# A selective-scan loop: rates spread from bf16 parts, both drives and both sums ahead of the rates in each step, and half of a convolution moved to VectorE

## What is computed

```python
xm, z = split(rmsnorm(x) @ W_in.T)
u     = silu(causal_depthwise_conv(xm, conv_w) + conv_b)      # 4 taps along the tokens
dt, Bm, Cm = split(u @ W_x.T)
delta = softplus(dt @ W_dt.T + b_dt)
A     = -exp(A_log)                                           # (512, 64)
for t in range(32):                                           # per sequence
    h = exp(delta[t][:, None] * A) * h + (delta[t] * u[t])[:, None] * Bm[t][None]
    y[t] = h @ Cm[t]
out = (y + u * Dp) * silu(z) @ W_out.T + x
```

## Time and profile before

| | us |
|---|---|
| median of 3 runs | 1955.35 (1955.21 to 1955.81) |
| the profiled execution | 1953.92 |
| its span, first to last instruction | 1952.1 |

### The profile page before, as it was taken

How to read it: one execution, slowest core, us unless ns; L and a number is a source line. 1 busy time by engine, 2 the same in 40 slices (tenths; PEclk the granted TensorE clock), 3 DMA queues, 4 the chain that set the end, 5 groups by cost and what they waited for, 6 DMA issues and landing times.

```text
span 1952.1 us, 24426 instructions
## 1 busy us (share of the span) xinstructions
PE 1711.4 (88%) x9096; PEld 821.3 (42%) x9096; DVE 1011.8 (52%) x1520; ACT 761.7 (39%) x1201; POOL 703.1 (36%) x430
## 2 busy tenths in 40 slices
PE   7888886898999999999997759999812979899998
PEld 4666663542322332332333525444401557644443
DVE  2444444255888888888884333222359464522121
ACT  1333332196676666666661222111413240112121
POOL 0433330215998998998995010000000014000000
PEclk8999997798999999999999768999865879789999
DMA  2111101002000100100100600111062100101110
GB/s 68 32 32 32 32 27 52 0 8 96 12 12 7 29 12 7 29 12 7 29 6 17 223 1 0 33 48 32 5 143 70 33 0 1 44 1 43 44 43 21
DMA packets 36491, 65.63 MB, mean 34 GB/s; under 512 B 13509, under 2 KB 22617, under 8 KB 34981
## 3 DMA queue, kind: packets, MB, share of 16 engines
q1 hardware_dynamic: 33204, 63.42, 11.0%
q10 hardware_dynamic: 3200, 1.07, 0.2%
HBM read 55.80 MB, written 8.67 MB: 33 GB/s over the span
## 4 chain that ended last, share of the span: by engine, by line
PE 80%; DVE 12%; ACT 2%; DMA 2%; issue 2%; POOL 1%; SPq 1%; DVEq 0%; ACTq 0%; POOLq 0%
PE ps L845 17%; PE ps L888 7%; PE ps L1376 6%; PE ps L2123 6%; PE ps L2112 6%; PE ps L860 5%; PE ps L201 4%; PE ps L1389 3%; PE ps L342 3%; PE ps L347 3%; PE ps L224 3%; PE ps L360 2%; DVE arena L477 2%; PE ps L1887 2%; PE ps L1903 2%
## 5 line engine op out<-in xcount | busy, mean ns | idle before, releaser
L1156 POOL TENSOR_TENSOR arena<-arena 128x768 f32<-128x768 f32 x248 | 521.5, 2122 | 75.2 <-DVE arena L1106 45.0
L845 PE MATMUL ps<-arena 32*128 32x512 f32 x2016 | 368.7, 647 | 2.9 <-DMA arena<-m_bd 2.9
L1106 DVE TENSOR_TENSOR arena<-arena,ps 128x1024 f32<-128x1024 f32 x248 | 302.0, 1218 | 11.7 <-POOL arena L1156 5.5
L845 PEld LDWEIGHTS ps<-arena 32*128 32x128 f32 x2016 | 130.0, 184 | 194.2 <-issue 165.2
L1086 DVE TENSOR_TENSOR arena<-arena,ps 128x1024 f32<-128x1024 f32 x124 | 151.4, 1221 | 87.5 <-PE ps L845 87.5
L1012 ACT ACTIVATE arena<-arena 128x1024 f32<-128x1024 f32 x124 | 131.0, 1057 | 166.1 <-DVE arena L1086 166.1
L2069 POOL TENSOR_TENSOR arena<-arena 128x1024 f32<-128x1024 f32 x16 | 29.9, 1896 | 435.0 <-DVE arena L2002 421.7
L888 PE MATMUL ps<-arena 128*32 128x512 f32 (+15 forms) x1024 | 136.2, 604 | 9.4 <-DVE arena L1106 8.9
L1019 ACT ACTIVATE arena<-ps 128x1024 f32<-128x1024 f32 x124 | 127.0, 1024 | 19.7 <-PE ps L845 3.4
L1021 ACT ACTIVATE arena<-arena 128x1024 f32<-128x1024 f32 x124 | 131.1, 1057 | 3.9
L1376 PE MATMUL ps<-arena 128*128 128x512 f32 x288 | 131.8, 602 | 0.6 <-ACT arena L1441 0.6
(11 more groups left out here) (291 smaller groups left out, 2345.3 us busy)
## 6 DMA issues: line engine op xcount, KB each, us to landing
arena<-ctxT SPq DMA_DIRECT2D x32, 257.0 KB, 3.0
arena<-ctxT SPq DMA_DIRECT2D x8, 1028.0 KB, 15.2
arena<-L_ffn_w SPq DMA_DIRECT2D x16, 512.0 KB, 4.3
arena<-ctx_rows SPq DMA_DIRECT2D x8, 960.0 KB
m_rows<-arena SPq DMA_DIRECT2D x16, 256.0 KB, 3.0
arena<-m_rows SPq DMA_DIRECT2D x64, 64.0 KB
arena<-L_ffn_eW SPq DMA_DIRECT2D x8, 512.0 KB, 3.5
m_yd<-arena SPq DMA_DIRECT2D x64, 32.0 KB, 2.3
```

What stands on the lines that cost most here:

```text
L845: mm = nc.tensor.matmul(ps[:, bank + jj, :], weights[r], m_row[r, n // CH % 2, n % CH, :], start=start, stop=True)
L1106: nc.vector.tensor_tensor(m_h[:, u, n % 2], m_xa[:, u, n % 2], ps[:, bank:bank + 2, :], ALU.add).then_inc(S["m_use"], 1)
L1156: nc.gpsimd.tensor_tensor(x, x, m_h[:, u, (n - 1) % 2].rearrange("p j d -> p (j d)")[:, own], ALU.mult).then_inc(S["m_kept"], 1)
```

## The change

Four things are done.

1. **Rates from bf16 parts.** Delta is cut into three bf16 parts that add up to it (`split`, ten GpSimd instructions per half of the tokens, five for each of two blocks q). The parts are written to HBM (`m_rbd`) and read into rows 0 to 5 and 32 to 37 of a new buffer `m_rb`, and one bf16 matmul against `m_selb`, a 0/1 matrix with ones at the rows of the parts, adds them. It takes the place of the fp32 matmul of `rates`. A chunk is twelve DMAs instead of six. GpSimd zeroes the new buffers (4096 bf16 columns each).
2. **The order in a step.** TensorE: drive(n, 0), drive(n, 1), read_out(n - 1), rates(n + 2), logs(n + 2). VectorE: carry(n), state(n, 0), state(n, 1), rate(n + 2). The ring of PSUM banks follows. GpSimd's and ScalarE's orders in the loop are what they were, and so is `SHARE`.
3. **Convolution of the second half** of the tokens on VectorE (one tensor_scalar and three scalar_tensor_tensor for each of four blocks) in place of 16 fp32 matmuls.
4. **The work ahead of the loop in another order**: max(x, 0) goes from ScalarE to VectorE, both halves' products with W_x and W_dt come together, the polynomials of the two halves are interleaved, and the second half's rows are written behind the issue of the first two chunks.

```diff
         for n in range(STEPS):
-            m_order += [("d0", n)] + [("r", n + 2)] * rated(n + 2) + [("d1", n)] + [("l", n + 2)] * rated(n + 2)
+            m_order += [("d0", n)] + [("d1", n)] + [("r", n + 2)] * rated(n + 2) + [("l", n + 2)] * rated(n + 2)
...
             def rates(n):
                 arrived(n)
-                spread(room(("r", n)), sel, n, 0)
+                bank = room(("r", n))
+                for jj in range(2):
+                    r = slice(32 * jj, 32 * jj + 32)
+                    mm = nc.tensor.matmul(ps[:, bank + jj, :], m_selb[r].rearrange("p s n -> p (s n)"),
+                                          m_rb[r, n // CH % 2, n % CH, :], start=True, stop=True)
+                mm.then_inc(S["m_fill"], 1)
...
             for n in range(STEPS):
                 drive(n, 0)
+                drive(n, 1)
                 if n:
                     read_out(n - 1)
                 if rated(n + 2):
                     rates(n + 2)
-                drive(n, 1)
                 if rated(n + 2):
                     logs(n + 2)
...
                 state(n, 0)
+                state(n, 1)
                 if rated(n + 2):
                     rate(n + 2)
-                state(n, 1)
...
+            def split(h):
+                for i in range(2):
+                    q = 4 * h + 2 * i
+                    n = 4 * (2 * h + i)
...
+                    nc.gpsimd.tensor_copy(m_part(h, i, 0), m_delta[:, q, :]).then_inc(S["m_cut"], 1)
...
+                    nc.gpsimd.tensor_tensor(m_rest(h), m_delta[:, q, :], m_part(h, i, 0), ALU.subtract).then_inc(S["m_cut"], 1)
...
+                    nc.gpsimd.tensor_copy(m_part(h, i, 1), m_rest(h)).then_inc(S["m_cut"], 1)
...
+                    nc.gpsimd.tensor_tensor(m_rest(h), m_rest(h), m_part(h, i, 1), ALU.subtract).then_inc(S["m_cut"], 1)
...
+                    nc.gpsimd.tensor_copy(m_part(h, i, 2), m_rest(h)).then_inc(S["m_split"], 1)
...
+            pool.wait_ge(*S.at("m_bmm", 1))
+            zeroed(0)
+            step_sizes(0)
+            split(0)
+            zeroed(1)
+            step_sizes(1)
+            pool.wait_ge(*S.at("m_ln", 2))
+            pool.wait_ge(*S.at("m_dudone", 4))
+            split(1)
...
+            for c in range(IC):
+                dve.wait_ge(*S.at("mi_ev_d", IC + c + 1))
...
+                ch.link(nc.vector.tensor_scalar(half(m_u, c, 1), half(m_xm, c, 1), m_cw[:, c, KW - 1:KW], None, ALU.mult))
+                for s in range(1, KW):
+                    ins = nc.vector.scalar_tensor_tensor(out=y3[:, :, s:], in0=x3[:, :, :L - s],
...
+            quadratics(0, 0, 5)
+            quadratics(1, 0, 2)
+            driven(0)
+            quadratics(1, 2, 5)
+            driven(1)
```

More of the change, by code:

```diff
@@ L608, in build, with m_part, m_rest @@
         m_Bc = view(25 * K, T)
-        m_du = [view(EXTRA, 4, DI)[:, q] for q in range(4)] + [view(24 * K, 4, DI)[:, q] for q in range(4)]
+        m_du = [view(EXTRA, 4, DI)[:, q] for q in range(4)] + [m_p[:, q] for q in (0, 2, 4, 6)]
+        m_selb = bview(TAIL + 2784, SEQS, NS)
+        m_rb = bview(22 * K, 2, 8, DI)
         FRONT = 30
+        def m_part(h, i, part):
+            return bview((18 if h else 26) * K + 768 * i + 256 * part, DI)
+        def m_rest(h):
+            return view((18 if h else 26) * K + 1536, DI)
         def m_sq(h, k):
@@ L665, in keep_row @@
             def keep_row(ty, q):
[L666 to L670, removed]
+                if ty == 0 and q % 2 == 0:
+                    sp.wait_ge(*S.at("m_split", q // 2 + 1))
+                    for part in range(3):
+                        sp.dma_start(m_rbd[part, 4 * q:4 * q + 4].rearrange("s t d -> (s t) d"),
+                                     m_part(q // 4, q // 2 % 2, part)).then_inc(S[f"m_st{q // 4}"], 16)
+                    return
+                sp.wait_ge(*(S.at("m_dudone", q + 1) if ty else S.at("m_ln", q // 2 + 1)))
                 sp.dma_start(m_rows[ty, 4 * q:4 * q + 4].rearrange("s t d -> (s t) d"),
-                             src).then_inc(S[f"m_st{q // 4}"], 16)
+                             m_du[q] if ty else m_p[:, q, :]).then_inc(S[f"m_st{q // 4}"], 16)
             def chunk(c):
@@ L701, in y_back @@
                         .then_inc(S[f"m_yb{g // 2}"], 16)
[L703 to L715, removed]
+            keep_b(0)
+            for q in (1, 3, 0, 2):
+                keep_row(0, q)
+            for q in range(4):
+                keep_row(1, q)
+            sp.wait_ge(*S.at("m_st0", 208))
+            sp.wait_ge(*S.at("mr_out", 4))
+            sp.wait_ge(*S.at("m_xused", 1))
+            chunk(0)
+            chunk(1)
+            keep_b(1)
+            for q in range(4, 8):
+                keep_row(1, q)
+            for q in (5, 7, 4, 6):
+                keep_row(0, q)
+            sp.wait_ge(*S.at("m_st1", 208))
             for c in range(2, GROUPS * NCH):
@@ L1006, in m_act @@
                     act.wait_ge(*S.at("mz_mm", 4 * h + i + 1))
[L1007 removed]
+                    nc.scalar.activation(half(m_z, i, h), ps[:, bank_of(0, i), :], ACT.Silu).then_inc(S["mz_ev"], 1)
             logged(1)
```

147 lines of the change are left out of this document (94 added, 53 removed).

## The result

| | before | after |
|---|---|---|
| median of 4 runs each, us | 1955.28 (1951.32 to 1955.81) | 2109.48 (2108.22 to 2111.44) |
| profiled execution, us | 1953.92 | 2108.99 |
| its span, us | 1952.1 | 2107.4 |
| state loop, first rate of VectorE to last state, us | 588.6 | 735.9 |
| one step of the loop, us | 4.57 | 5.82 |

A forecast was written before the change was run, and what follows sets the result against it. A circle through state, read-out, rates and VectorE's rate was taken to bound the kernel, 4.57 us a step. A blocked small carry, +150, and +11 ahead of the loop gave 1955.35 + 161 = 2116 us, range 2075 to 2150.

The forecast's parts named there:

- The circle and what is late next: State loop: new order takes read-out and rates out of the circle; GpSimd's pair is next, 4.22 us a step without contention.
- TensorE's circle: State loop before: state(n - 1, 1), read-out, rates, VectorE's rate, state(n, 1) form a circle of 4.57 us a step.
- The small carry: VectorE's 256-column carry in the loop: issued 0.28 us late, waits out GpSimd's long carry; step 5.80 us, +150 us.
- Rivals 1: State loop: no block worth speaking of, step 4.22, loop -42, ahead +3, 1916 us; chance 0.06.
- 2: State loop: block lasts only for a part, small carry 0.78, step 4.38, about 1938 us; chance 0.06.
- 3: State loop: small carry slips in ahead of GpSimd's long one, +0.5 a step, 2026 us; chance 0.03.
- The clock: TensorE in the state loop: its clock should stay at 1.00.
- Rival 4: TensorE's clock falls in a quarter of the loop, steps there some 7.9 us, +65, 2180 us; chance 0.03.
- Ahead of the loop: Work before the state loop: +3 us undisturbed, up to +11 more if VectorE blocks GpSimd; +11 taken, range 3 to 15.
- the memset: GpSimd's zeroing ahead of the loop: costs nothing if it ends before delta's polynomial does, 3.8 us if not.

The follow-up runs named there:

- experiment 2: Changed kernel with VectorE's small carry replaced by a sum of neighbouring pairs, one SBUF input, outputs wrong: 1906.57 us in a single run.
- experiment 4: Changed kernel with the order in a step (part 2) undone, parts 1, 3 and 4 kept: 1927.49 us, ratio 0.9881 to the kernel before.
- experiment 9: Changed kernel with VectorE's last three polynomial instructions of the second half held until the first half is split: 2104.43 us, ratio 1.0767 to the kernel before.
- 5: Changed kernel, new order kept, with the next step's small carry placed between state(n, 0) and state(n, 1): 1932.87 us, ratio 0.9899 to the kernel before.

## Why the prediction was right

The forecast was 2116 us in 2075 to 2150, slower; 2109.5 was measured. Term by term:

- **The circle and what is late next: right.** Without contention a step was to take 4.22; with the second SBUF input gone it took 4.19 (experiment 2), GpSimd being the bound. TensorE's circle of the earlier trace rows was indeed broken, but the bf16 rates do that without the new order (experiment 4).
- **The small carry: right in place, mechanism and size.** The mean was to be 2.3 and is 2.313; the step was to be 5.80 and is 5.82; GpSimd's idle time 1.6 and is 1.68; the loop +150 and is +147.3. It rested on one instruction in each group of 32 steps that took 0.78 for 0.42, and on noting that it ended 0.3 behind GpSimd's. Those rows showed 0.3 to 0.5 us of such a wait; in the kernel after it lasts for 2 us, and ends only behind GpSimd's instruction, so here nothing was given up within an instruction. The Trainium skill, SBUF — State Buffer, section Who interferes with whom, says so of the shared pair of ports, and the trace agrees (issued at 704.83, done 0.29 us behind the end of GpSimd's pair; 2.39 with two SBUF inputs, 0.41 with one). Rivals 1, 2 and 3 are excluded by the mean.
- **The clock: right.** It is 0.99 of full speed over the loop in both kernels (the prediction said 1.00), with gaps of 1.14 us in TensorE's work in each step. Rival 4 did not come.
- **Ahead of the loop: near in sum, its parts mis-sized both ways.** The loop's first matmul came 9.1 us later (453.18 to 462.25), forecast +11. Of the 11, 3 were work without disturbance and 8 the block by VectorE (the text names up to 11 for it, but takes 11 in all). Against that: the block added 6.0 to the split (10.4 against 4.4) and 2.6 to the deltas (7.58 against 4.96), 8.6, so +0.6. A cast undisturbed takes 0.61, not the 0.9 that I took between a memset and a subtraction, so the split of both blocks costs 8.9 undisturbed (two times 4.43) instead of 11: -2.1. From the end of the split (446.12) to the chunk's issue it took 5.8 us instead of 6.6, and from there to the first matmul 10.3 instead of 11.2 (today's 7.9 and 3.3): -0.8 and -0.9. The step that failed is that the memset "ends before delta's polynomial does": it waited until 420.18, took 3.51 and ended at 423.69, while the polynomial's last instruction ended at 419.77 + 2.29 = 422.06. So the first delta started at 423.65 instead of the forecast 422.4: +1.2. The sum is 11 + 0.6 - 2.1 - 0.8 - 0.9 + 1.2 = 9.0. That the total came within 2 us of the forecast is in part luck, since the misses cancelled.

What stays open: the convolution on VectorE (part 3) was not run alone. Experiment 4 has it with part 1 and part 4, at -29 in the loop. Its first rate comes only 5.7 us later than before, but the layer began sooner in that execution:

```profile
386.25 3.67 PE L765 MATMUL ps<-arena 128*128 128x512 f32 x8 [0.87 <-ACT arena L965]
```

From this product to the first rate it took 73.8 us, the kernel after 73.6 and the kernel before 65.4. So the work ahead of the loop costs some 8 us in both, as its code is the same. How the 8 us divide among the three parts isn't shown, beyond the 5 to 6 us that the disturbed split costs (experiment 9).

## What to carry to other kernels

Before an instruction is moved within one engine's order, ask what the other engine is in the middle of at the new place. In this loop the VectorE instruction with two SBUF inputs was short in GpSimd's gap (0.42 us) or at a border between two of its instructions (0.48 and 0.67); some 0.3 us too late it had to wait out the whole of GpSimd's instruction (2.39), and the loop became 25% longer. Look for the one odd duration of a repeated instruction (0.78 among 0.42): it is the experiment that the kernel before has already made. And a busy share that rises with the same number of instructions can be a wait; here it was one.

## What the runs showed of the hardware

- The time for which VectorE is held by GpSimd is recorded as busy time of its instruction, with 0.0 of idle ahead. In the loop VectorE reads as 98% busy (718.8 of 736), some 230 us of which is waiting.
- A VectorE instruction that already waits gets in between two GpSimd instructions that follow each other without a pause: it took 0.67 us in experiment 4 and 0.48 in 5, at the price of 0.19 us on the GpSimd instruction behind it (2.56 for 2.37, 2.01 for 1.82). What decides who goes first at such a border isn't shown.
- GpSimd's memset, which reads nothing, took 3.51 us beside VectorE's two-input instructions (420.18, above) and 3.51 again at 446.18, with VectorE idle, while casts and subtractions of GpSimd were held for 1.9 to 2.2 us by the same kind of instruction.
